# Two moves in the order of VectorE and ScalarE in a two-layer graph kernel

## The chip, the core and the metric

The kernel runs on one core of one Trainium2 chip. The metric is the device time of one launch in microseconds (us): the three runs of the kernel before gave 996.67, 996.7 and 994.24, median 996.67. The engines are named as the profile names them: PE is TensorE (PEld its weight loads), DVE is VectorE, ACT is ScalarE, POOL is GpSimd, SP is SyncE, which only issues transfers. Each engine runs its own instructions strictly in their order and waits on semaphores for the others.

## The reference

Inputs: x (8 x 2048 x 128), adj (2048 x 2048), W0 (128 x 128), W1 (3 x 128 x 128), bias (128), all fp32.

```
h = relu(layernorm(x))
A = relu((adj + adj.T) / 2);  d = rowsum(A) ** -0.5
x = x + relu(h @ W0 - d * (A @ (d * (h @ W0))))          # layer 0, per batch
h = relu(layernorm(x))
x = x + diag(adj) * (h @ W1[0]) + triu(adj, 1) @ (h @ W1[1])
      + tril(adj, -1) @ (h @ W1[2]) + bias               # layer 1, per batch
```

Layer 0 multiplies a symmetric 2048 x 2048 matrix by 8 batches of 2048 x 128, layer 1 does it with the two triangles of adj.

## The kernel before

**Tiling.** The 2048 rows are 16 strips of 128, the 8 batches two halves of 4, so one strip of one half is a tile of 128 x 512. A matmul in fp32 is split in three: each operand is written as a high part (suffix h, rounded to the fast type) and a low part (suffix l, the rest), and high x high, high x low and low x high are summed.

**Stages.** After a first phase (sums of rows and columns, h of half 0 and its product with W0) a step body runs 64 times, c = 0 to 63. A step makes one output strip of one half: 16 blocks k of three matmuls each into psAcc (lines 490 to 492), 48 in all. Steps 0 to 15 are layer 0 of half 0, 16 to 31 layer 0 of half 1, 32 to 47 and 48 to 63 layer 1 of the two halves. The matrix strip of a step comes in four quarters q of 128 x 512: C (from adj, or from DRAM once it is summed), Lh its high part (ACT, split_hi), Ll its low part (DVE, split_lo). In steps 0 to 15 PE also transposes adj (psA), ACT copies it (copy_T, AT), and DVE adds it to C (sum_T).

**Side work of a step.** PE does it between the blocks, in `finish(t, k)`:

- k = 3, steps 1 to 16: the transposed and normalised strip of half 1, yTh and yTl, times W0 into psW. ACT and DVE scale it into Yh and Yl.
- k = 7, steps 2 to 33: h2, the normalised result of the step before, is transposed into psZ (semaphore hT). ACT copies it into hTh (semaphore hThi), DVE makes hTl from psZ and hTh (hTlo).
- k = 11, steps 0 to 15: xp, a strip of half 1 that ACT has normalised (p_h), is transposed into the same psZ, and becomes yTh (ACT) and yTl (DVE). From step 2 on the transposes wait for hThi and hTlo.
- k = 11 and k = 14, steps 2 to 33: hTh and hTl times the three weights W1 into psG, 128 x 384 for each batch b. Batches 0 and 1 come at k = 11, 2 and 3 at k = 14. psG has two banks, b % 2, so batch 2 waits until bank 0 has been read (semaphore gev), batch 3 until bank 1 has.

**Who reads psG.** DVE adds the first 128 columns, times the diagonal, to x1: `t_out(t, b)`, line 797, semaphore tev. It waits for g_ok of the batch. ACT then copies the other 256 columns into g12: `gev_out(t, b)`, line 585, semaphore gev. It waits for tev of the same batch. t_dram and g_dram take both to DRAM for layer 1. The bias was added to x1 by POOL (xb_ok).

**The order around the change** is written out by hand in the bodies of ACT and DVE. ACT, in steps 2 to 15: split_hi, relu of z into x1 (line 611), Yh (614), normalisation of xp in four pieces (620), hTh (627), copy_T 1, split_hi 1, copy_T 2, the load of the next xp (638), yTh (640), gev_out 0 and 1, split_hi 2, h2 (651), gev_out 2 and 3. From step 16 on `prep(t)` (line 674) stands in the place of the xp normalisation: it copies xp, which then comes from g_dram, into the high operand of layer 1. DVE: x1 plus xe (840), Yl (844), hTl (849), sum_T 1, statistics of x1 (695 to 702), split_lo 1, yTl (859), t_out 0 and 1, sum_T 2, the negated mean (705), t_out 2 and 3.

Of the kernel before, what the change touches and what calls it, by code (L numbers as in the profile page):

```python
# [6 lines left out]
F32 = mybir.dt.float32  # L7
F32R = mybir.dt.float32r
ALU = mybir.AluOpType
ACT = mybir.ActivationFunctionType  # L10
# [4 lines left out]
NB = N // P  # L15
# [5 lines left out]
L1 = 2 * NB  # L21
# [19 lines left out]
def wait(eng, sem, value):  # L41

    if isinstance(value, int) and value <= 0:
        return
    eng.wait_ge(sem, value)
# [24 lines left out]
def build(nc, x, adj, w_l0, w_l1, bias, out):  # L70
# [12 lines left out]
    with ctx:  # L83
        def sb(name, shape, dt=F32, at=ctx):
            return at.enter_context(nc.sbuf_tensor(name, shape, dt))

        def sems(*names):
            return [ctx.enter_context(nc.semaphore(n)) for n in names]
# [26 lines left out]
        with ExitStack() as layer0:  # L115
# [8 lines left out]
        yTh, yTl = sb("yTh", [P, W], F32R), sb("yTl", [P, W], F32R)  # L124
        hTh, hTl = sb("hTh", [P, W], F32R), sb("hTl", [P, W], F32R)
# [22 lines left out]
        psZ = ctx.enter_context(nc.psum_tensor("psZ", [P, W], F32))  # L148
# [22 lines left out]
        yT, yThi, yTlo, yw_ok = sems("yT", "yThi", "yTlo", "yw_ok")  # L171
        cur_ok, hsum, z_ok, r1_ok, x1_ok = sems("cur_ok", "hsum", "z_ok", "r1_ok", "x1_ok")
        e_st, e_mv, e_ve, e_rs, e_nm, h2_ok, hT, hThi, hTlo = sems(
            "e_st", "e_mv", "e_ve", "e_rs", "e_nm", "h2_ok", "hT", "hThi", "hTlo")
        xb_ok, g_ok, gev, tev = sems("xb_ok", "g_ok", "gev", "tev")
# [20 lines left out]
        def blocks(ap):  # L196
            return ap.rearrange("p (b f) -> p b f", f=F)

        def strip(dram, s, back, q=None):

            a = dram[bass.ds(s.of(1, -back), 1)].rearrange("o p m -> (o p) m")
            return a if q is None else a[:, q * Q:(q + 1) * Q]
# [307 lines left out]
        def _(act):  # L510
            A = nc.scalar.activation
# [23 lines left out]
            def copy_T(s, q):  # L535

                wait(act, rT, s.of(4, q + 1))
                if q == 0:
                    wait(act, st_at[s.c % 2], s.pair(0, 16))
                A(AT[:, s.c % 2, q * Q:(q + 1) * Q], psA[:, q % 2, :], ACT.Copy).then_inc(at_ok, 1)  # L540

            def split_hi(s, q):

                if s.c < NB:
                    wait(act, S_ok, s.of(4, q + 1))
                else:
                    wait(act, ld_c[q], s.of(16, 16))
                if s.c:
                    wait(act, used, s.of(16, -16 + 4 * q + 4))
                A(Lh[:, q, :], C[:, q, :], ACT.Relu if s.c < L1 else ACT.Copy).then_inc(lhi, 1)  # L550
                if s.c < NB:
                    act.dma_start(strip(s_dram, s, 0, q), C[:, q, :]).then_inc(st_s[q], 16)
# [35 lines left out]
            def body(t):  # L588
                c = t.c
                pe_ = (c - 1) % 2  # L590
                nxt = Step(t.i, c + 1)
                if c:
                    split_hi(t, NQ - 1)
                if c >= L1:
                    wait(act, ld_lx, t.of(16, 16 * (1 - L1)))
                    wait(act, acc1, t.of(1, -L1))
                    A(lxh[:, :], lx[:, :], ACT.Copy).then_inc(lxh_ok, 1)
                    wait(act, ld_g2, t.of(16, 16 * (1 - L1)))
                    wait(act, slot_hi, t.of(1, -L1))
                    A(g2h[:, :], g2[:, :], ACT.Copy).then_inc(g2h_ok, 1)  # L600
                if c < NB - 1:
                    copy_T(nxt, 0)
                if c < LAST - 1:
                    split_hi(nxt, 0)
                if 1 <= c <= L1:
                    wait(act, z_ok, t.of(1, 0))
                    if c >= 3:
                        wait(act, st_t[pe_], t.pair(-1, 16))
                    elif c == 1:
                        act.wait_ge(wlo_ok, 1)  # L610
                    A(x1[:, pe_, :], z[:, :], ACT.Relu, scale=cur_e[:, 2:3]).then_inc(r1_ok, 1)
                if 1 <= c <= NB:
                    wait(act, yw_ok, t.of(1, 0))
                    A(Yh[:, bass.ds(t.of(1, -1), 1), :], psW[:, :].rearrange("p (o w) -> p o w", o=1), ACT.Copy,
                      scale=cur_e[:, 0:1]).then_inc(prep_hi, 1)
                if c < NB:
                    wait(act, p_nm, t.of(1, 1))
                    for b in range(HB):
                        f = slice(b * F, (b + 1) * F)
                        last = A(xp[:, f], xp[:, f], ACT.Relu, bias=npn.nm[:, b:b + 1], scale=npn.rs[:, b:b + 1])  # L620
                    last.then_inc(p_h, 1)
                elif c < L1 + NB:
                    prep(t)
                if 2 <= c < L1 + 2:
                    wait(act, hT, t.of(1, -1))
                    wait(act, g_ok, t.of(4, -8))
                    A(hTh[:, :], psZ[:, :], ACT.Copy).then_inc(hThi, 1)
                if c < NB - 1:
                    copy_T(nxt, 1)
                if c < LAST - 1:  # L630
                    split_hi(nxt, 1)
                if c < NB - 1:
                    copy_T(nxt, 2)
                if c < NB:
                    wait(act, yT, t.of(1, 1))
                    wait(act, yw_ok, t.of(1, 0))
                    if c < NB - 1:
                        act.dma_start(blocks(xp[:, :]), xv[1, bass.ds(t.of(1, 1), 1)]
                                      .rearrange("o p b f -> (o p) b f")).then_inc(ld_xp, 16)
                    A(yTh[:, :], psZ[:, :], ACT.Copy).then_inc(yThi, 1)  # L640
                if 2 <= c < L1 + 2:
                    gev_out(t, 0)
                    gev_out(t, 1)
                if c < LAST - 1:
                    split_hi(nxt, 2)
                if 1 <= c <= L1:
                    wait(act, e_nm, t.of(1, 0))
                    wait(act, hT, t.of(1, -1))
                    for b in range(HB):
                        f = slice(b * F, (b + 1) * F)  # L650
                        last = A(h2[:, f], x1[:, pe_, f], ACT.Relu, bias=ne.nm[:, b:b + 1], scale=ne.rs[:, b:b + 1])  # L651
                    last.then_inc(h2_ok, 1)
                if 2 <= c < L1 + 2:
                    gev_out(t, 2)
                    gev_out(t, 3)
                if c >= L1:
                    slot(t)
                if c < NB - 1:
                    copy_T(nxt, 3)
                if 2 <= c < L1 + 2:  # L660
                    wait(act, tev, t.of(4, -8 + 4))
                    act.dma_start(strip(t_dram, t, 2), x1[:, c % 2, :]).then_inc(st_t[c % 2], 16)
                    wait(act, gev, t.of(4, -8 + 4))
                    act.dma_start(strip(g_dram, t, 2), g12[:, :, :].rearrange("p k w -> p (k w)")).then_inc(st_g, 16)

            def prep(t):

                c = t.c
                dst, _ = half_of(c + NB)
                wait(act, ld_xp, t.of(16, 16))  # L670
                act.wait_ge(used, NB * (c // NB) * NB)
                wait(act, hsum, t.of(1, 1 - NB))
                off = t.of(1, -(c // NB) * NB)
                A(dst[:, bass.ds(off, 1), :], xp[:, :].rearrange("p (o w) -> p o w", o=1), ACT.Copy).then_inc(prep_hi, 1)  # L674

            def slot(t):
# [6 lines left out]
                  ACT.Copy).then_inc(slot_hi, 1)  # L683

            run_steps(act, body)


        @block.vector
        def _(dve):
            V = nc.vector  # L690
# [102 lines left out]
            def t_out(t, b):  # L793

                f = slice(b * F, (b + 1) * F)
                wait(dve, g_ok, t.of(4, -8 + b + 1))
                V.scalar_tensor_tensor(out=x1[:, t.c % 2, f], in0=psG[:, b % 2, 0:F], scalar=cur_g[:, 3:4],  # L797
                                       in1=x1[:, t.c % 2, f], op0=ALU.mult, op1=ALU.add).then_inc(tev, 1)

            def body(t):  # L800
                c = t.c
# [52 lines left out]
                    stats(ne, x1[:, pe_, :], e_st, e_mv, e_ve, t.of(1, 0))  # L854
                if c < LAST - 1:
                    split_lo(nxt, 1)
                if c < NB:
                    wait(dve, yThi, t.of(1, 1))
                    V.tensor_tensor(yTl[:, :], psZ[:, :], yTh[:, :].bitcast(F32), ALU.subtract).then_inc(yTlo, 1)
                if 2 <= c < L1 + 2:  # L860
                    wait(dve, xb_ok, t.of(1, -1))
                    t_out(t, 0)
                    t_out(t, 1)
                if c < NB - 1:
                    sum_T(nxt, 2)
                if 1 <= c <= L1:
# [150 lines left out]
```

## Time and profile before

| what | value |
|---|---|
| median of 3 runs | 996.67 us |
| lowest and highest | 994.24, 996.7 us |
| profiled execution | 995.62 us |
| its span | 993.9 us |
| PE busy | 940.1 us (95%) |
| DVE busy | 570.6 us (57%) |
| ACT busy | 501.3 us (50%) |
| POOL busy | 289.3 us (29%) |
| transfers | 213.73 MB, mean 215 GB/s |
| chain that ended last | PE 84%, issue 5%, ACT 3%, POOL 3% |

How to read it: busy time is the time in which an engine works on an instruction. A PE that is busy 95% of the span leaves little to win by faster work on the other engines; what counts there is where PE waits. The waits below are put down to the engine whose event came last. Releasers are inferred. In rows that merge several instructions, x4 is their number and the second column is the time from the first one's start to the last one's end. `[0.75 <-ACT g L585]` at a row's end is the idle time of the engine before it and what ended it. The profile writes x for x1, g for g12 and h for h2.

### The profile page before, as it was taken

How to read it: one execution, taken by the hardware profiler on the slowest of the kernel's cores; microseconds unless marked ns; L12 is line 12 of the kernel's file. 1: busy time of each engine (PE TensorE's matmuls, PEld its weight loads, DVE VectorE, ACT ScalarE, POOL GpSimd, SP SyncE). 2: the span in 40 equal slices, each digit the busy share in tenths (PEclk: the TensorE clock that was granted, in tenths of full speed). 3: DMA queues.
4: the chain of work that ended last, by engine and by line, in shares of the span. 5: the costliest groups of instructions: out<-in, count | busy, mean ns of one | idle time of the engine just before them, and what ended most of it. 6: DMA issues, size and time to landing. Idle time of an engine off the chain costs nothing.

```text
span 993.9 us, 17630 instructions
## 1 busy us (share of the span) xinstructions
PE 940.1 (95%) x4614; PEld 790.7 (80%) x4614; DVE 570.6 (57%) x1491; ACT 501.3 (50%) x1058; POOL 289.3 (29%) x289
## 2 busy tenths in 40 slices
PE   4787799999999999999999999999999999999998
PEld 4776688878878788888888887788888888888886
DVE  5996777667677676656666655453333433334342
ACT  5986566666656665445454554443343433333331
POOL 4776143433434334344443442111111100000000
PEclk9877899999999999999999999999999999999999
DMA  8995689889998987556565555675666655555552
GB/s 234 320 331 158 200 286 309 306 294 299 306 320 287 310 302 237 173 153 171 171 190 169 171 158 181 181 222 182 187 188 187 193 169 160 170 162 168 168 156 75
DMA packets 181210, 213.73 MB, mean 215 GB/s; under 512 B 13616, under 2 KB 116016, under 8 KB 178992
## 3 DMA queue, kind: packets, MB, share of 16 engines
q1 hardware_dynamic: 154816, 167.36, 55.8%
q10 hardware_dynamic: 26352, 45.88, 12.9%
q8 instruction: 18, 0.29, 0.1%
q14 instruction: 24, 0.20, 0.1%
HBM read 145.04 MB, written 68.16 MB: 215 GB/s over the span
## 4 chain that ended last, share of the span: by engine, by line
PE 84%; issue 5%; ACT 3%; POOL 3%; DVE 2%; DMA 1%; ACTq 1%; SPq 0%; DVEq 0%; POOLq 0%
PE psAcc L490 21%; PE psAcc L492 21%; PE psAcc L491 21%; PE psG L461 3%; PE psA L392 3%; PE psG L463 2%; PE psG L462 2%; PE psZ L423 2%; POOL colacc L918 2%; PE psA L404 1%; ACT yTh L640 1%; PE psW L364 1%; POOL n_rs L910 1%; PE psW L363 1%; PE psAcc L504 1%
## 5 line engine op out<-in xcount | busy, mean ns | idle before, releaser
L550 ACT ACTIVATE Lh<-C 128x512 fp32r<-128x512 f32 x256 | 161.4, 631 | 286.3 <-PE psAcc L492 236.2
L490 PE MATMUL psAcc<-Xh,Lh 128*128 128x512 f32 x512 | 208.0, 406 | 5.4 <-DVE Xl L777 4.7
L492 PE MATMUL psAcc<-Xh,Ll 128*128 128x512 f32 x512 | 201.9, 394 | 0.0
L491 PE MATMUL psAcc<-Xl,Lh 128*128 128x512 f32 x512 | 201.5, 394 | 0.0
L490 PE MATMUL psAcc<-Yh,Lh 128*128 128x512 f32 x512 | 200.9, 392 | 0.0
L492 PE MATMUL psAcc<-Yh,Ll 128*128 128x512 f32 x512 | 200.3, 391 | 0.0
L491 PE MATMUL psAcc<-Yl,Lh 128*128 128x512 f32 x512 | 200.0, 391 | 0.0
L721 DVE TENSOR_TENSOR Ll<-C,Lh 128x512 fp32r<-128x512 f32 x128 | 90.8, 711 | 143.6 <-ACT Lh L550 143.5
L490 PEld LDWEIGHTS psAcc<-Xh,Lh 128*128 128x128 f32 x512 | 97.7, 191 | 23.7 <-issue 6.3
L492 PEld LDWEIGHTS psAcc<-Xh,Ll 128*128 128x128 f32 x512 | 97.1, 190 | 21.3
L492 PEld LDWEIGHTS psAcc<-Yh,Ll 128*128 128x128 f32 x512 | 96.1, 188 | 20.2
L491 PEld LDWEIGHTS psAcc<-Xl,Lh 128*128 128x128 f32 x512 | 97.8, 191 | 17.8
L491 PEld LDWEIGHTS psAcc<-Yl,Lh 128*128 128x128 f32 x512 | 96.2, 188 | 18.9
L490 PEld LDWEIGHTS psAcc<-Yh,Lh 128*128 128x128 f32 x512 | 96.2, 188 | 18.7
L718 DVE SCALAR_TENSOR_TENSOR Ll<-C,Lh 128x512 fp32r<-128x512 f32 x128 | 95.9, 749 | 22.2 <-ACT Lh L550 19.6
L585 ACT ACTIVATE g<-psG 128x256 f32<-128x256 f32 x128 | 43.0, 377 | 68.4 <-DVE x L797 67.6
L976 POOL TENSOR_TENSOR x<-x,biasb 128x512 f32<-128x512 f32 x32 | 44.1, 1379 | 99.6 <-ACT h L651 99.6
L970 POOL TENSOR_TENSOR Yl<-xp,Yh 128x512 f32 (+1 forms) x16 | 20.7, 1292 | 162.6 <-ACT Yh L674 162.6
L910 POOL TENSOR_TENSOR ne_rs<-ne_ve,mhalf 128x4 f32<-128x4 f32 x32 | 44.8, 1400 | 75.5 <-DVE ne_ve L702 75.5
L797 DVE SCALAR_TENSOR_TENSOR x<-psG,cur_g,x 128x128 f32<-128x128 f32 x128 | 42.1, 347 | 40.0 <-PE psG L463 39.6
L712 DVE TENSOR_TENSOR C<-AT,C 128x512 f32<-128x512 f32 x64 | 46.9, 733 | 22.3 <-ACT AT L540 22.3
L540 ACT ACTIVATE AT<-psA 128x512 f32<-128x512 f32 x64 | 37.6, 590 | 43.2 <-PE psA L392 43.2
(124 smaller groups left out, 1469.8 us busy)
## 6 DMA issues: line engine op xcount, KB each, us to landing
C<-at_dram SPq DMA_DIRECT2D x128, 256.0 KB, 2.7
at_dram<-AT SPq DMA_DIRECT2D x16, 1088.0 KB, 5.5
R<-in_adj SPq DMA_DIRECT2D x64, 256.0 KB, 6.4
C<-in_adj SPq DMA_DIRECT2D x64, 256.0 KB, 4.8
s_dram<-C ACTq DMA_DIRECT2D x64, 256.0 KB, 4.3
g_dram<-g ACTq DMA_DIRECT2D x32, 512.0 KB, 4.2
C<-s_dram SPq DMA_DIRECT2D x64, 256.0 KB, 3.7
xe<-in_x SPq DMA_DIRECT2D x32, 256.0 KB, 3.7
```

The lines of the kernel that those rows point to most:

```text
L490: mm(acc, lh, rh[:, k, :], start=k == 0, stop=False)
L491: mm(acc, lh, rl[:, k, :], start=False, stop=False)
L492: mm(acc, ll, rh[:, k, :], start=False, stop=c < L1 and k == NB - 1).then_inc(used, 1)
L540: A(AT[:, s.c % 2, q * Q:(q + 1) * Q], psA[:, q % 2, :], ACT.Copy).then_inc(at_ok, 1)
L550: A(Lh[:, q, :], C[:, q, :], ACT.Relu if s.c < L1 else ACT.Copy).then_inc(lhi, 1)
L585: A(g12[:, :, b * F:(b + 1) * F], psG[:, b % 2, F:3 * F].rearrange("p (k f) -> p k f", k=2), ACT.Copy).then_inc(gev, 1)
L712: V.tensor_tensor(C[:, q, :], AT[:, s.c % 2, q * Q:(q + 1) * Q], C[:, q, :], ALU.add).then_inc(S_ok, 1)
L718: V.scalar_tensor_tensor(out=Ll[:, q, :], in0=C[:, q, :], scalar=0.0, in1=Lh[:, q, :].bitcast(F32), op0=ALU.max, op1=ALU.subtract).then_in ...
L721: V.tensor_tensor(Ll[:, q, :], C[:, q, :], Lh[:, q, :].bitcast(F32), ALU.subtract).then_inc(llo, 1)
L797: V.scalar_tensor_tensor(out=x1[:, t.c % 2, f], in0=psG[:, b % 2, 0:F], scalar=cur_g[:, 3:4], in1=x1[:, t.c % 2, f], op0=ALU.mult, op1=ALU ...
L910: return G.tensor_tensor(out=out, in0=base, in1=exponent, op=ALU.pow)
L976: G.tensor_tensor(out=blocks(x1[:, pe_, :]), in0=blocks(x1[:, pe_, :]), in1=biasb[:, :].unsqueeze(1).to_broadcast([P, HB, F]), op=ALU.add) ...
```

## The change

On ACT, the copy hTh moves ahead of the normalisation of xp (steps 2 to 15) and so ahead of `prep(t)` (steps 16 to 33). On DVE, t_out 0 and 1 move ahead of yTl in steps 2 to 15. From step 16 on yTl does not exist and DVE's order is the old one. No instruction is added or taken away, and every wait goes with its instruction.

```
@@ -613,6 +613,10 @@  (ScalarE)
+                if 2 <= c < L1 + 2:
+                    wait(act, hT, t.of(1, -1))
+                    wait(act, g_ok, t.of(4, -8))
+                    A(hTh[:, :], psZ[:, :], ACT.Copy).then_inc(hThi, 1)
                 if c < NB:
                     wait(act, p_nm, t.of(1, 1))
                     for b in range(HB):
...
                     last.then_inc(p_h, 1)
                 elif c < L1 + NB:
                     prep(t)
-                if 2 <= c < L1 + 2:
-                    wait(act, hT, t.of(1, -1))
-                    wait(act, g_ok, t.of(4, -8))
-                    A(hTh[:, :], psZ[:, :], ACT.Copy).then_inc(hThi, 1)
                 if c < NB - 1:
                     copy_T(nxt, 1)
@@ -854,13 +854,13 @@  (VectorE)
                 if c < LAST - 1:
                     split_lo(nxt, 1)
-                if c < NB:
-                    wait(dve, yThi, t.of(1, 1))
-                    V.tensor_tensor(yTl[:, :], psZ[:, :], yTh[:, :].bitcast(F32), ALU.subtract).then_inc(yTlo, 1)
                 if 2 <= c < L1 + 2:
                     wait(dve, xb_ok, t.of(1, -1))
                     t_out(t, 0)
                     t_out(t, 1)
+                if c < NB:
+                    wait(dve, yThi, t.of(1, 1))
+                    V.tensor_tensor(yTl[:, :], psZ[:, :], yTh[:, :].bitcast(F32), ALU.subtract).then_inc(yTlo, 1)
                 if c < NB - 1:
                     sum_T(nxt, 2)
```

VectorE in step 2, from the statistics of x1 to split_lo of quarter 2, before (x<-psG is t_out, C<-AT is sum_T, Ll is split_lo):

```order
L699 BN_AGGR ne_mv<-ne_st 128x2 x4
L702 TENSOR_SCALAR ne_ve<-ne_mv 128x4
L718 SCALAR_TENSOR_TENSOR Ll<-C,Lh 128x512
L859 TENSOR_TENSOR yTl<-psZ,yTh 128x512
L797 SCALAR_TENSOR_TENSOR x<-psG,cur_g,x 128x128 x2
L712 TENSOR_TENSOR C<-AT,C 128x512
L705 SCALAR_TENSOR_TENSOR ne_nm<-ne_mv,ne_rs 128x4
L797 SCALAR_TENSOR_TENSOR x<-psG,cur_g,x 128x128 x2
```

The same place after the change:

```order
L699 BN_AGGR ne_mv<-ne_st 128x2 x4
L702 TENSOR_SCALAR ne_ve<-ne_mv 128x4
L718 SCALAR_TENSOR_TENSOR Ll<-C,Lh 128x512
L797 SCALAR_TENSOR_TENSOR x<-psG,cur_g,x 128x128 x2
L863 TENSOR_TENSOR yTl<-psZ,yTh 128x512
L712 TENSOR_TENSOR C<-AT,C 128x512
L705 SCALAR_TENSOR_TENSOR ne_nm<-ne_mv,ne_rs 128x4
L797 SCALAR_TENSOR_TENSOR x<-psG,cur_g,x 128x128 x2
```

The first pair of t parts has changed places with yTl; the second pair stays.

ScalarE in step 2, from the relu to the first copies of psG, before (AT<-psA is copy_T, Lh is split_hi, g<-psG is gev_out):

```order
L611 ACTIVATE x<-z,cur_e 128x512
L614 ACTIVATE Yh<-psW,cur_e 128x512
L620 ACTIVATE xp<-xp,np_nm,np_rs 128x128 x4
L627 ACTIVATE hTh<-psZ 128x512
L540 ACTIVATE AT<-psA 128x512
L550 ACTIVATE Lh<-C 128x512
L552 DMA s_dram<-C 128x512
L540 ACTIVATE AT<-psA 128x512
L638 DMA xp<-in_x 128x4x128
L640 ACTIVATE yTh<-psZ 128x512
L585 ACTIVATE g<-psG 128x2x128 x2
```

The same place after the change, its first five instructions:

```order
L611 ACTIVATE x<-z,cur_e 128x512
L614 ACTIVATE Yh<-psW,cur_e 128x512
L619 ACTIVATE hTh<-psZ 128x512
L624 ACTIVATE xp<-xp,np_nm,np_rs 128x128 x4
L540 ACTIVATE AT<-psA 128x512
```

hTh now stands ahead of the four pieces of xp; what follows is unmoved.

## Rows read from the trace of the kernel before

**Rows 1.** Busy time of each engine: us, share of the span, instructions.

```profile
PE 940.1 (95%) x4614; PEld 790.7 (80%) x4614; DVE 570.6 (57%) x1491; ACT 501.3 (50%) x1058; POOL 289.3 (29%) x289
```

**Rows 2.** Waits, 136 to 390 us: engine, line, releaser: us, times, longest.

```profile
ACT AT L540 <- PE psA L392: 34.3, 26, 1.8
...
PE psG L461 <- ACT g L585: 9.1, 13, 0.8
PEld psZ L423 <- issue: 5.6, 11, 0.7
...
ACT x L611 <- DMA t_dram<-x: 2.0, 1, 2.0
...
DVE x L840 <- DMA xe<-in_x: 0.4, 1, 0.4
```

**Rows 3.** Timeline of PE, step 11, k = 14: start, us, instruction.

```profile
314.97 0.39 PE L492 MATMUL psAcc<-Xh,Ll 128*128 128x512 f32 x1
316.11 0.44 PE L461 MATMUL psG<-Wh,hTh 128*128 128x384 f32 x1 [0.75 <-ACT g L585]
316.38 0.33 PE L462 MATMUL psG<-Wl,hTh 128*128 128x384 f32 x1
```

**Rows 4.** Timeline of PE at the same place in step 19.

```profile
443.20 0.39 PE L492 MATMUL psAcc<-Yh,Ll 128*128 128x512 f32 x1
443.43 0.33 PE L461 MATMUL psG<-Wh,hTh 128*128 128x384 f32 x1
443.61 0.34 PE L462 MATMUL psG<-Wl,hTh 128*128 128x384 f32 x1
```

**Rows 5.** Timeline of ACT and DVE, step 11, around yTl.

```profile
313.98 0.60 ACT L640 ACTIVATE yTh<-psZ 128x512 fp32r<-128x512 f32 x1
...
314.61 0.69 DVE L859 TENSOR_TENSOR yTl<-psZ,yTh 128x512 fp32r<-128x512 f32 x1 [0.92 <-ACT yTh L640]
...
315.22 0.60 DVE L797 SCALAR_TENSOR_TENSOR x<-psG,cur_g,x 128x128 f32<-128x128 f32 x2
...
315.67 0.66 ACT L585 ACTIVATE g<-psG 128x256 f32<-128x256 f32 x2 [1.09 <-DVE x L797]
```

**Rows 6.** Timeline of ACT and DVE, step 11, around hTh.

```profile
308.18 1.64 ACT L620 ACTIVATE xp<-xp,np_nm,np_rs 128x128 f32<-128x128 f32 x4
...
309.72 0.58 ACT L627 ACTIVATE hTh<-psZ 128x512 fp32r<-128x512 f32 x1
...
310.33 0.69 DVE L849 TENSOR_TENSOR hTl<-psZ,hTh 128x512 fp32r<-128x512 f32 x1 [1.13 <-ACT hTh L627]
```

**Rows 7.** Timeline of PE, step 11, k = 11.

```profile
310.65 0.39 PE L492 MATMUL psAcc<-Xh,Ll 128*128 128x512 f32 x1
311.17 0.63 PE L423 MATMUL psZ<-ident,xp 128*128 128x128 f32 x4
```

**Rows 8.** Waits, 390 to 660 us.

```profile
ACT Xh L674 <- DMA xp<-g_dram: 26.8, 13, 3.4
...
PE psG L461 <- ACT hTh L627: 2.2, 1, 2.2
PE psG L461 <- DVE hTl L849: 1.0, 2, 0.8
```

**Rows 9.** Busy time by stretch: length, engines (instructions), granted clock, DMA share, GB/s.

```profile
308.30:309.30 1.00, 1.00 (x7) 0.79 (x6) 0.89 (x2) 1.00 (x3) 1.00 (x1) 1.00 0.06 12
...
312.30:313.30 1.00, 1.00 (x9) 0.97 (x8) 0.86 (x7) 0.07 (x1) 0.13 (x1) 1.00 1.21 426
...
620.93:624.35 3.42, 3.42 (x10) 2.82 (x9) 1.73 (x9) 2.05 (x6) 1.39 (x1) 0.51 0.33 97
```

**Rows 10.** Transfers, 136.24 to 373.35 us, all queues.

```profile
DMA packets 61043, 71.54 MB, mean 302 GB/s; under 512 B 3499, under 2 KB 42975, under 8 KB 59369
```

**Rows 11.** DMA issues, 300 to 318.9 us: KB each, us to landing.

```profile
xp<-in_x ACTq DMA_DIRECT2D x1, 256.0 KB, 6.5
```

**Rows 12.** Timeline of DVE, step 12: the statistics of xp.

```profile
320.62 0.86 DVE L695 BATCH_NORM_STATS2 np_st<-xp 128x6 f32<-128x128 f32 x4
```

More of the change, by code:

```diff
@@ L615, in body @@
                       scale=cur_e[:, 0:1]).then_inc(prep_hi, 1)
+                if 2 <= c < L1 + 2:
+                    wait(act, hT, t.of(1, -1))
+                    wait(act, g_ok, t.of(4, -8))
+                    A(hTh[:, :], psZ[:, :], ACT.Copy).then_inc(hThi, 1)
                 if c < NB:
@@ L623, in body @@
                     prep(t)
[L624 to L627, printed above, removed]
                 if c < NB - 1:
@@ L856, in body @@
                     split_lo(nxt, 1)
-                if c < NB:
-                    wait(dve, yThi, t.of(1, 1))
-                    V.tensor_tensor(yTl[:, :], psZ[:, :], yTh[:, :].bitcast(F32), ALU.subtract).then_inc(yTlo, 1)
                 if 2 <= c < L1 + 2:
@@ L863, in body @@
                     t_out(t, 1)
+                if c < NB:
+                    wait(dve, yThi, t.of(1, 1))
+                    V.tensor_tensor(yTl[:, :], psZ[:, :], yTh[:, :].bitcast(F32), ALU.subtract).then_inc(yTlo, 1)
                 if c < NB - 1:
```

## The prediction

> **What bounds the kernel now.** I read the busy times first. TensorE is busy 940.1 of 993.9 us [rows 1], so a change on VectorE or ScalarE pays only where TensorE waits. I split the span by step: one execution of the step body, which gives one strip of 128 rows of the result. The layer-0 steps c = 2 to 14 lie between 136.24 and 373.35 us, 13 steps of 18.24 us each. The steps from c = 34 on take about 11.6 us, and no moved instruction is in them. The waits of the stage come second [rows 2]. The reader should look for lines that start with PE or PEld, since the others are waits of engines that have time. Two matter. PE waits 9.1 us in 13 pieces for ACT's copy out of psG (L585), one piece per step. The weight loader stands idle 5.6 us in 11 pieces ahead of the transposes of xp (L423). "Issue" there means that the view names no releaser; I look for it below. The third view is the timeline of one step, c = 11, from 300 to 318 us.
>
> **Part 1, the t parts ahead of yTl on VectorE.** The chain is: t part b=0 (DVE L797) raises tev, ACT may then copy the same psG bank (L585), and PE may then write block b=2 into that bank (L461, at k = 14). Before, the last accumulating matmul starts at 314.97 and L461 at 316.11, which is 1.14 us later [rows 3]. Undisturbed, this pair is 0.23 us apart, and L462 follows L461 after 0.18, where behind the stall it takes 0.27 [rows 4]. A stall therefore costs more than the idle time shown: 1.14 - 0.23 = 0.91 against 0.75 shown, so 0.16 more, and 0.09 behind it.
> In [rows 5] DVE has nothing to do for 0.92 us before yTl: it waits for ACT's yTh (313.98 to 314.58), then does yTl (314.61 to 315.30), then the two t parts, and ACT's psG copies start at 315.67. The t parts need none of this. Their matmuls on b=0 and b=1 ended before 313. In the new order they run from about 313.6 to 314.2, inside the 0.92 us of idle time (0.60 us of work), and yTl still starts when yTh is done, at 314.6. So yTl pays nothing, and the sum_T behind it comes 0.4 us earlier. ACT finds tev raised when it is through with yTh, and copies b=0 from about 314.5 to 314.85. Before, PE's weight load started about 0.1 us after that copy; now it may start at 314.95, and PE is ready for it at about 315.2 (314.97 + 0.23). The stall goes, with a margin of 0.25 us. The second copy ends about 315.2 and is wanted at 315.8. What is late next at this place is yTh itself, which sits behind ACT's AT copy, and that copy waits for PE (the 34.3 us line of [rows 2]), so it moves along with PE.
> Term A: 9.1 + 13 x 0.16 + 13 x 0.09 = 12.4 us. Bounds: 0 if the wait only changes its name, 12.4 if it goes whole.
> Behind the stall ACT works without a gap until about 319.8 and can start only some 0.6 us earlier, not 1.0. It then has its waits for PE's transposes (34.3 us in the stage, 2.6 us per step), and they cover the 0.4 us.
>
> **Part 2, hTh ahead of the normalisation of xp on ScalarE, c < 16.** ACT runs relu x1, Yh, the four xp pieces (308.18 to 309.82) and then hTh (309.72 to 310.30); DVE waits 1.13 us and does hTl, 310.33 to 311.02 [rows 6]. PE's transposes of xp write psZ, which hTl reads, so they wait for it: the matmul before starts at 310.65 and the first transpose at 311.17, 0.52 us later [rows 7], against 0.23 undisturbed. The weight load follows hTl's end by 0.12 us. That is the "issue" of [rows 2].
> New: hTh at 308.2 to 308.8 (its source, the transposes of h2, is there by 307.9), xp from 308.7 to 310.3, hTl right behind Yl at about 309.1 to 309.8. PE then waits for xp: 310.3 + 0.12 = 310.4, wanted at 310.65. Margin 0.2 us, nothing paid for moving xp back by 0.5 us. ACT's total is the same, so its AT copy at 310.20 stays.
> Term B: 11 x 0.29 = 3.2 us. Bounds: if xp is late by the whole 0.5 us in every step, -13 x 0.3 = -3.9; if not, +3.2. I take 3.2, since the xp end is read from rows and only shifted by one copy.
>
> **Part 3, the same move in c = 16 to 33, ahead of the copy of the h operand (L674).** That copy waits up to 3.4 us for its DMA, with hTh behind it [rows 8]. PE shows this twice, 1.0 us in all; with 0.16 + 0.09 each 1.5 us. Once hTh goes first it is ready at its transposes' end, over 1 us before PE needs it. The L674 copy starts up to 0.6 us later in steps where its data are early. What waits for it is POOL's low part, which is needed only in the next stage. Term C: 1.5 us. At c = 32 PE waits 2.2 us for hTh [rows 8], but ACT is late there because of the g2 load; only the 0.6 us copy is taken out of its way, and DVE is not free for all of that. Term D: 0.3 us, bounds 0 and 0.6. Behind this wait the clock fell to half for 3.4 us (0.51 granted, [rows 9]), so 1.7 us more are possible if the shorter wait avoids it. I leave that out of the sum and keep it for the low end.
>
> **Transfers.** They are the cover that may go. The 13 steps move 71.54 MB at 302 GB/s [rows 10], 5.5 MB a step. At 18.24 - 1.2 = 17.0 us that is 323 GB/s. Single microseconds reach 426 GB/s, and there are holes with 12 [rows 9], about 2 us per step, so the same transfers fit in some 16.3 us.
> The Trainium skill (HBM Reference, the per-core bandwidth at its top) says a core alone streams at about 425 GB/s and that its share is about 358 when its neighbour streams too. The 426 above agrees with a core alone. By 425 a step's transfers would take 12.9 us, by 358 they would take 15.4, and both are under 17.0; the page speaks against the DMA rival below.
> Single landings are tight all the same. xp is issued at 313.51 and lands 6.5 us later [rows 11], 0.6 us before its statistics start at 320.62 [rows 12], and that interval shrinks by about 1.0. DVE then waits 0.4 us there, but it waits for an AT copy a little later in any case, which covers it. xe has some 2 us, t_dram's store 1.5; each has failed once already, 0.4 and 2.0 us [rows 2]. Term E: -1.5 us, an allowance for one or two such waits. Bounds 0 and -8.
>
> **Sum.** 12.4 + 3.2 + 1.5 + 0.3 - 1.5 = 15.9 us. The profiled execution took 995.62 us (span 993.9 and 1.7 around it) and would take 979.7. It lies 1.05 under the median of the three runs; from 996.67 the same sum gives 980.8. I predict 981.
>
> **Rivals.**
> (1) Transfers or a tight landing give part back. For it: the 302 GB/s mean of the stage [rows 10], and SP's queue, which waits for s_dram stores before it loads the next C. Against: the holes. If each of 13 steps loses 0.5 us, the time is 981 + 6.5 = 987.5, near 988.
> (2) The margins of 0.2 us do not hold: yTh or xp ends just late, and PE waits for them instead. A wait of 0.3 us with its 0.25 of extra in each of 13 steps, at one of the two places, gives 7 us back: also 988. At both places: 995, no change.
> (3) The change does not do what it says at L461, because PE's wait hangs on something other than tev, such as the g_dram store that the b=0 copy also waits for. Against: that store is issued about 301.1 and lands 5 to 6 us later, long before 314.5. Only B, C and D would be left: 996.7 - 5 = 992.
> (4) Slower: SP's queue becomes the bound. It is in order, so a late s_dram store holds up xe and the loads behind it; a late xe holds up DVE, hence hTl and PE. It decides when the landing times of 4.7 to 6.5 us grow by over 2 us. To end above 999.7 it must take back the 17.4 and 3 more, 1.6 us in each step, so a step of 18.6 us with less data in flight than now. The price is possible, the profile gives it little.
>
> **Chances.** Forecast (976 to 984.5) 0.66; rivals 1 and 2 (984.5 to 990) 0.22; rival 3 and larger parts of 1 and 2 (990 to 993.7) 0.06; no change 0.03; slower 0.03. The 0.3% that a measurement of this kernel tells from no change is 3 us. Faster: 0.66 + 0.22 + 0.06 = 0.94. The range 976 to 989 leaves out the upper cases, about 0.14, and a little at the low end: C, A and B whole, no allowance and the clock kept gives 996.67 - 17.4 - 1.7 = 977.6.
>
> **What the profile after should show.** The line PE psG L461 <- ACT g gone or under 2 us, yTl's wait for yTh down from 0.92 to about 0.3 us per step, the psG copies right behind yTh; hTl without its wait for hTh in both stages; the load before the xp transposes without its "issue"; steps of about 17.0 us; 320 GB/s or more over the stage. Wrong if: PE waits for ACT xp L624 or ACT yTh in most steps (rival 2), new DMA waits on DVE L840, L695 or ACT L611 (rival 1), or the L461 wait stays (rival 3). If steps are 17.0 us and the total is not 14 us or more lower, the loss is in the stages I took as unchanged.

## The result and the profile after

| kernel | median, us | lowest to highest | ratio to before, 95% interval |
|---|---|---|---|
| before | 996.35 (4 runs) | 994.24 to 996.7 | 1 |
| changed | 978.35 (4 runs) | 977.53 to 980.24 | 0.9826 (0.9806 to 0.9847) |

The change takes 18.0 us off. The forecast was 981, with 976 to 989 as the range. In a second set of runs, on another chip, the changed kernel stood at 977.21 against 996.9, ratio 0.9797 (0.9773 to 0.9821).

The profiled execution of the changed kernel took 980.24 us, the slowest of its four, with a span of 978.5. Before it was 995.62 and 993.9. So the two traces differ by 15.4 us and the medians by 18.0. The difference is cut up below by the start of `z` (DVE L813) or of the result (L891), which happens once in each step.

| stretch, us | before | changed | difference |
|---|---|---|---|
| first phase and step 0 | 120.57 | 121.89 | +1.32 |
| step 1 | 15.67 | 15.69 | +0.02 |
| steps 2 to 14 | 237.11 | 222.83 | -14.28 |
| steps 15 to 31 | 236.91 | 235.01 | -1.90 |
| steps 32 and 33 | 38.18 | 37.46 | -0.72 |
| steps 34 to 63 | 341.80 | 342.00 | +0.20 |

The sum is -15.4. The first row is scatter, not the change: over the twelve profiles of this study, none of whose edits touches the first phase, it lies between 117.8 and 123.1 us. What an edit does is therefore read from the stretches, and the total only from the runs.

The busy times of the changed kernel answer to [rows 1]. PE is busy 6.5 us less, at the same share of 95%. Of this 4.8 us lie in steps 2 to 14, where the matmul before a stall is counted to its own end (0.39 us) and not to the next start (0.23 us), and 1.8 us in steps 32 and 33, where the kernel before had 3.4 us at the lower clock.

```profile
PE 933.6 (95%) x4614; PEld 793.2 (81%) x4614; DVE 568.6 (58%) x1491; ACT 504.1 (52%) x1058; POOL 285.7 (29%) x289
```

The waits of the changed kernel from 136 to 373 us (engine, line, releaser: us, times, longest) answer to [rows 2]:

```profile
ACT AT L540 <- PE psA L392: 27.5, 26, 1.6
...
DVE yTl L863 <- ACT yTh L640: 3.6, 13, 0.4
DVE x L840 <- DMA xe<-in_x: 2.7, 3, 0.9
...
DVE np_st L695 <- DMA xp<-in_x: 1.6, 3, 0.9
...
ACT x L611 <- DMA t_dram<-x: 1.4, 1, 1.4
...
PEld psZ L423 <- ACT xp L624: 1.1, 1, 1.1
PE psZ L423 <- DVE hTl L849: 0.9, 2, 0.7
```

PE's 9.1 us for the psG copies are gone, and so is the "issue" ahead of L423 but for one. yTl's wait is 3.6 us, 0.28 a step. DVE waits longer for transfers, 2.7 us for xe where it was 0.4, and two of these waits reach PE, in steps 5 and 7 (0.68 and 0.20 us of idle time at L423); the wait for xp L624 is in step 5 too.

The timeline of the changed kernel at k = 14 of step 11 (start, us, instruction) answers to [rows 3, 5]:

```profile
305.19 0.60 DVE L797 SCALAR_TENSOR_TENSOR x<-psG,cur_g,x 128x128 f32<-128x128 f32 x2
305.37 0.60 ACT L640 ACTIVATE yTh<-psZ 128x512 fp32r<-128x512 f32 x1
305.86 0.66 ACT L585 ACTIVATE g<-psG 128x256 f32<-128x256 f32 x2
306.00 0.69 DVE L863 TENSOR_TENSOR yTl<-psZ,yTh 128x512 fp32r<-128x512 f32 x1 [0.20 <-ACT yTh L640]
...
306.37 0.40 PE L492 MATMUL psAcc<-Xh,Ll 128*128 128x512 f32 x1
306.60 0.34 PE L461 MATMUL psG<-Wh,hTh 128*128 128x384 f32 x1
306.77 0.34 PE L462 MATMUL psG<-Wl,hTh 128*128 128x384 f32 x1
```

The t parts run beside yTh, the psG copies start 0.49 us after yTh does instead of 1.69, and L461 follows L492 after 0.23 instead of 1.14. L462 follows after 0.17, not 0.27.

The timeline of the same step around k = 11 answers to [rows 6, 7]:

```profile
299.88 0.59 ACT L619 ACTIVATE hTh<-psZ 128x512 fp32r<-128x512 f32 x1
...
300.35 1.65 ACT L624 ACTIVATE xp<-xp,np_nm,np_rs 128x128 f32<-128x128 f32 x4
...
300.81 0.68 DVE L849 TENSOR_TENSOR hTl<-psZ,hTh 128x512 fp32r<-128x512 f32 x1
...
302.35 0.40 PE L492 MATMUL psAcc<-Xh,Ll 128*128 128x512 f32 x1
302.58 0.49 PE L423 MATMUL psZ<-ident,xp 128*128 128x128 f32 x3
```

hTh is done at 300.47. hTl no longer waits for it, only for DVE's own Yl, and is done at 301.49. xp is done at 302.00, 0.35 us before the last matmul ahead of the transposes starts, and the transposes come 0.23 after that matmul. With the 0.12 us that the prediction puts between an operand's end and the weight load, the margin is 0.23 us.

Busy time by stretch for the changed kernel: length, PE, PEld, DVE, ACT, POOL (instructions), granted clock, DMA share, GB/s. The next row is its transfer total over steps 2 to 14; it answers to [rows 10].

```profile
137.58:360.41 222.83, 221.95 (x1247) 192.95 (x1246) 171.02 (x507) 146.14 (x312) 90.34 (x117) 1.00 0.95 322
360.41:595.42 235.01, 235.01 (x1122) 199.89 (x1121) 144.88 (x406) 125.25 (x266) 98.37 (x74) 1.00 0.59 179
```

```profile
DMA packets 61123, 71.71 MB, mean 322 GB/s; under 512 B 3505, under 2 KB 42973, under 8 KB 59449
```

The same 71.7 MB go through in 222.8 us. In steps 15 to 31 PE's busy time equals the length of the stretch.

### The profile page after: what moved, and what is told of

It is laid out like the page before. It is cut to its first block, busy times and chain, and to the rows that moved or that the text cites. A ratio compares the mean times of both kernels' runs of the same rounds, so it can differ in the third digit from the quotient of the medians.

```text
span 978.5 us, 17630 instructions
## 1 busy us (share of the span) xinstructions
PE 933.6 (95%) x4614; PEld 793.2 (81%) x4614; DVE 568.6 (58%) x1491; ACT 504.1 (52%) x1058; POOL 285.7 (29%) x289
## 4 chain that ended last, share of the span: by engine, by line
PE 84%; issue 4%; DMA 3%; DVE 3%; ACT 3%; POOL 1%; SPq 0%; ACTq 0%; DVEq 0%; POOLq 0%
PE psAcc L492 22%; PE psAcc L490 22%; PE psAcc L491 22%; PE psA L392 2%; PE psG L461 2%; PE psG L463 2%; PE psG L462 2%; PE psZ L423 2%; DMA s_dram<-C 1%; DMA xe<-in_x 1%; PE psA L404 1%; ACT hst L521 1%; PE psAcc L504 1%; PE psAcc L503 1%; PE psAcc L502 1%
## 5 line engine op out<-in xcount | busy, mean ns | idle before, releaser
L492 PE MATMUL psAcc<-Xh,Ll 128*128 128x512 f32 x512 | 201.1, 393 | 0.0
L492 PE MATMUL psAcc<-Yh,Ll 128*128 128x512 f32 x512 | 200.1, 391 | 0.0
L492 PEld LDWEIGHTS psAcc<-Xh,Ll 128*128 128x128 f32 x512 | 96.8, 189 | 21.2
L492 PEld LDWEIGHTS psAcc<-Yh,Ll 128*128 128x128 f32 x512 | 96.1, 188 | 20.2
L976 POOL TENSOR_TENSOR x<-x,biasb 128x512 f32<-128x512 f32 x32 | 41.9, 1308 | 91.9 <-ACT h L651 91.9
L891 DVE TENSOR_TENSOR x<-psAcc,x 128x512 f32<-128x512 f32 x32 | 22.1, 691 | 59.7 <-PE psAcc L504 46.6
```

What stands on the lines that cost most here:

```text
L492: mm(acc, ll, rh[:, k, :], start=False, stop=c < L1 and k == NB - 1).then_inc(used, 1)
L891: V.tensor_tensor(x1[:, pp, :], psAcc[:, pp, :], x1[:, pp, :], ALU.add).then_inc(o_ok, 1)
L976: G.tensor_tensor(out=blocks(x1[:, pe_, :]), in0=blocks(x1[:, pe_, :]), in1=biasb[:, :].unsqueeze(1).to_broadcast([P, HB, F]), op=ALU.add) ...
```

## The experiments

All ratios are to the kernel before on the same chip. Two numbers are counted from each trace over steps 2 to 14. "k = 14" is the sum of the start-to-start times L492 to L461 above 0.23 us, plus those of L461 to L462 above 0.18. "k = 11" is the sum of L492 to L423 (xp) above 0.23. The kernel before had 996.16 on the chip of the next four rows after "changed", 994.82 on that of the four after them, and 996.9 on that of the last two, so medians of different chips are compared through the ratio.

| kernel | median | ratio (95%) | steps 2 to 14 | k = 14 | k = 11 | steps 15 to 31 | 32 and 33 |
|---|---|---|---|---|---|---|---|
| before | 996.35 | 1 | 237.11 | 12.4 | 3.0 | 236.91 | 38.18 |
| changed | 978.35 | 0.9826 (0.9806 to 0.9847) | 222.83 | 0 | 1.2 | 235.01 | 37.46 |
| VectorE part alone | 982.04 | 0.9862 (0.9841 to 0.9883) | 224.78 | 0 | 3.1 | 237.34 | 37.01 |
| ScalarE part alone | 989.59 | 0.9947 (0.9926 to 0.9967) | 233.86 | 12.4 | 0 | 235.01 | 36.48 |
| old order from step 16 | 980.98 | 0.9849 (0.9826 to 0.9873) | 221.76 | 0 | 0.1 | 237.56 | 37.18 |
| yTh in 4 pieces | 976.95 | 0.9809 (0.9787 to 0.9831) | 223.44 | 0 | 2.1 | 235.01 | 37.01 |
| yTh in 8 pieces | 980.77 | 0.9862 (0.9843 to 0.9880) | 224.02 | 2.8 | 0.3 | 234.98 | 36.20 |
| xe loaded early | 978.01 | 0.9828 (0.9808 to 0.9848) | 221.59 | 0 | 0 | 235.02 | 37.44 |
| lxh, g2h late | 975.03 | 0.9810 (0.9791 to 0.9829) | 222.60 | 0 | 1.0 | 235.02 | 34.87 |
| the last two together | 974.29 | 0.9801 (0.9783 to 0.9819) | 221.65 | 0 | 0 | 235.02 | 34.90 |
| changed, again | 977.21 | 0.9797 (0.9773 to 0.9821) | 221.85 | 0 | 0.3 | 235.02 | 36.30 |
| the last two, again | 975.47 | 0.9784 (0.9759 to 0.9808) | 221.66 | 0 | 0 | 235.02 | 35.15 |

**The VectorE part alone.**

```
-                if c < NB:
-                    wait(dve, yThi, ...); V.tensor_tensor(yTl...)
                 if 2 <= c < L1 + 2:
                     wait(dve, xb_ok, t.of(1, -1))
                     t_out(t, 0)
                     t_out(t, 1)
+                if c < NB:
+                    wait(dve, yThi, ...); V.tensor_tensor(yTl...)
```

> Only the first two t parts move ahead of yTl on VectorE; ScalarE as before. My theory (two independent stalls of TensorE per step, one at k = 14 behind the psG copies, one at k = 11 behind hTl): the k = 14 stall goes, 12.4 us less than before over steps 2 to 14, the k = 11 stall stays at 0.2 to 0.3 us a step. About 984 to 985 us; PE psG L461 <- ACT g under 1 us in the stage, DVE hTl <- ACT hTh unchanged near 15 us. Rival (the two moves need each other, since either stall alone can hold the step): less than half of it, 990 or more, with the k = 11 wait grown to 0.8 us or more a step.

Measured: 982.04 us, steps 2 to 14 shorter by 237.11 - 224.78 = 12.33 us, the 12.4 that was expected. The total is 2 us below what was expected, within its interval (0.9841 to 0.9883 is 4 us wide). The k = 11 stall is untouched. Its waits, 136 to 362 us:

```profile
DVE hTl L849 <- ACT hTh L627: 12.7, 11, 1.2
...
PEld psZ L423 <- issue: 5.7, 11, 0.8
```

The rival, that one stall alone can hold the step, falls: at k = 11 PE waits as long as before, 3.1 against 3.0 us.

**The ScalarE part alone.** The changed ScalarE with the old VectorE, so the diff is the first hunk of the change.

> Only hTh moves ahead on ScalarE; VectorE as before. My theory: terms B, C and D alone, 3.2 + 1.5 + 0.3 to 0.7 us, so 991 to 992 us; the k = 14 stall stays at 0.7 to 0.9 us in 13 steps. Rival (what PE gains at k = 11 it loses at k = 14, because the psG copies hang on VectorE's yTl and do not move): the steps 2 to 14 stay at 18.2 us and only C and D are left, 994 to 995 us; the k = 14 stall would then grow to about 1.1 us.

Measured: 989.59 us. Steps 2 to 14 are 3.25 us shorter, and the k = 11 stall is down from 3.0 to 0. The k = 14 stall has not grown (12.4 both times), so the rival that PE loses there what it gains at k = 11 falls. The stretches show 3.25 + 1.90 + 1.70 = 6.9 us; 991 to 992 was expected. The two last steps gave more than the 0.3 to 0.7 expected. Its waits, 136 to 375 us:

```profile
PEld psG L461 <- ACT g L585: 14.6, 13, 1.2
...
PE psG L461 <- ACT g L585: 8.9, 13, 0.8
```

The parts add up but for the late landings: 12.33 + 3.25 = 15.58 alone, 14.28 together, and the missing 1.3 is the k = 11 column of the changed kernel (1.2).

**The old order from step 16.**

```
+                if 2 <= c < NB:
+                    ... hTh
                 if c < NB:
                     ... xp
                 elif c < L1 + NB:
                     prep(t)
+                if NB <= c < L1 + 2:
+                    ... hTh
```

> The changed kernel, but from step 16 on hTh stands behind the copy of the h operand again. My theory: steps 2 to 14 as in the changed kernel (17.1 us each), steps 15 to 31 give back 1.5 to 1.9 us, and at c = 32 the wait of PE for hTh is 2.2 us again, with the half clock behind it (up to 1.7 us): 980 to 982 us. Rival (the later part of the move is worth nothing and the gain there was a chance of landing times): 978 to 979 us, and steps 15 to 31 as long as in the changed kernel.

Measured: 980.98 us, steps 15 to 31 at 237.56, 2.55 us longer than in the changed kernel. Each kernel with the new order from step 16 has 235.0 there (nine profiles, 234.98 to 235.02), and each without it 236.9 to 237.6 (three profiles). The rival falls. PE's waits of this kernel, 390 to 660 us:

```profile
PE psG L461 <- ACT hTh L631: 2.0, 1, 2.0
...
PE psG L461 <- DVE hTl L853: 1.1, 3, 0.5
```

The 2.0 us wait at step 32 is back as expected, but no half clock follows it, and steps 32 and 33 take 37.18 us, no longer than in the changed kernel.

**yTh in four pieces.** A delay of the psG copies without other work:

```
-                    A(yTh[:, :], psZ[:, :], ACT.Copy).then_inc(yThi, 1)
+                    for k in range(4):
+                        f = slice(k * 128, (k + 1) * 128)
+                        last = A(yTh[:, f], psZ[:, f], ACT.Copy)
+                    last.then_inc(yThi, 1)
```

> The changed kernel with the copy yTh cut into four pieces of 128 columns, so that it ends later by some 0.3 us (if a piece takes 0.23) to 1.0 us (if it takes the 0.4 of the xp pieces), and the psG copies behind it too. The margin at k = 14 was forecast as 0.25 us. My theory: with a delay of d the stall is back at d - 0.25 a step plus 0.25 of extra once it exists, so for d = 0.3 about 0.3 x 13 = 4 us (982), for d = 1.0 about 13 us (991). Rival (the margin is much larger, since PE is not at L461 before 315.5): no change for d = 0.3, 978 to 979.

Measured: the four pieces take 0.79 us, and the psG copies start 0.65 us after yTh does instead of 0.49. So d is 0.16, less than either case the expectation gave, and inside the margin: no stall at k = 14, no change of time. By itself it decides nothing.

**yTh in eight pieces** of 64 columns, the same edit.

> The changed kernel with the copy yTh cut into eight pieces of 64 columns. Cut into four it cost 0 to 0.2 us of PE's margin at k = 14 and no time. Eight pieces at the same step should end about 0.8 us later than the one copy. My theory (margin 0.25 us, then the stall is back): about 0.5 us a step in 13 steps, 6 to 8 us more than the changed kernel, 984 to 986 us, with PE psG L461 <- ACT g back in 12 or 13 steps. Rival (PE has much more room there): 978 to 979 us and no such wait.

Measured: 1.04 us for the eight, the psG copies 0.84 us after the start of yTh, so d is 0.35. The stall is back in the ten steps of the loop, the steps with the small margin. Its timeline, step 11:

```profile
304.47 1.04 ACT L642 ACTIVATE yTh<-psZ 128x64 fp32r<-128x64 f32 x8
305.31 0.75 ACT L585 ACTIVATE g<-psG 128x256 f32<-128x256 f32 x2
...
305.46 0.40 PE L492 MATMUL psAcc<-Xh,Ll 128*128 128x512 f32 x1
305.83 0.44 PE L461 MATMUL psG<-Wh,hTh 128*128 128x384 f32 x1
306.12 0.34 PE L462 MATMUL psG<-Wl,hTh 128*128 128x384 f32 x1
```

L461 comes 0.37 us after L492, 0.14 late, and L462 0.11 late behind it. So the margin is 0.35 - 0.14 = 0.2 us; 0.25 was forecast. The cost is 2.8 us by the k = 14 column and 3.6 by the ratios (0.9862 against 0.9826, whose intervals just overlap). The 6 to 8 expected was wrong mainly in d, taken as 0.8. The price of a step was taken as d - 0.25 and is d - 0.2 + 0.1, in ten steps and not 13.

**xe loaded early.** SP asks for xe right after the store of AT, ahead of the loads for the step after next:

```
+                if c < L1:
+                    step_wait(sp, x1_ok, t.of(1, 0))
+                    ... sp.dma_start(xe)
                 for q in range(1, NQ):
                     if c < LAST - 2:
                         load_next(Step(t.i, c + 2), q - 1)
...
-                    if q == 2 and c < L1:
-                        ... the same load
```

> The changed kernel with the load of xe issued by SP ahead of two loads of the step after next (R and C of quarters 0 and 1), some 8 us earlier. My theory (what is left over 17.0 us in steps 5 and 7 is a late xe): DVE x <- DMA xe gone, steps 5 and 7 as long as their neighbours, steps 2 to 14 down from 222.8 to 221.5 us, total 1 to 1.5 us less: 977. Rival (the transfers as a whole are the limit, and xe only the one that shows): another landing takes its place, xp or t_dram, and steps 2 to 14 stay at 222.8 or above.

In the changed kernel, step 5, the chain from xe to PE reads (timeline; the add L840 itself takes 1.15 us here and 0.69 in step 11, of which more in the last section):

```profile
197.06 1.15 DVE L840 TENSOR_TENSOR x<-x,xe 128x512 f32<-128x512 f32 x1 [0.93 <-DMA xe<-in_x]
...
198.80 0.67 DVE L849 TENSOR_TENSOR hTl<-psZ,hTh 128x512 fp32r<-128x512 f32 x1
...
199.62 0.63 PE L423 MATMUL psZ<-ident,xp 128*128 128x128 f32 x4 [0.68 <-DVE hTl L849]
```

With the early load the only wait for a transfer left from 136 to 375 us is this, and it reaches nobody:

```profile
DVE np_st L695 <- DMA xp<-in_x: 0.8, 2, 0.5
```

Steps 2 to 14 are 221.59 us and the k = 11 column is 0, as in both other profiles with this edit. The six with the VectorE and the ScalarE part and xe in its old place have 0.1 to 2.1 there, so the chain is shown, and what it costs differs from one execution to the next. The rival falls too, since nothing took its place. In the total the version can't be told from the changed kernel (978.01, ratio 0.9828 against 0.9826).

**lxh and g2h late**, in steps 32 and 33 only: on ScalarE both copies move behind hTh, on VectorE lxl and g2l behind hTl.

```
-                if c >= L1:
+                if c >= L1 + 2:
                     ... lxh, g2h       (lxl, g2l on VectorE)
...
+                if L1 <= c < L1 + 2:
+                    ... lxh, g2h       (lxl, g2l, behind hTl)
```

> The changed kernel with the copies of the diagonal block and of g2 (lxh, g2h on ScalarE, lxl, g2l on VectorE) behind hTh and hTl in steps 32 and 33 only. My theory (TensorE waits at k = 11 of these two steps because hTh stands behind copies that wait for a load issued at the step's start): the waits of 1.5 and 1.1 us go, steps 32 and 33 together 37.5 to 35 us, total 2 to 2.5 us less, 976. Rival (the same loads gate the end of the step, so that the wait only moves there): the two steps stay at 37 us or more.

Measured: 975.03 us, the two steps at 34.87 instead of 37.46. In the changed kernel hTh started at 602.83 only, behind copies that had waited 4.8 us for lx, and PE stood 1.45 us at L461. Of PE's waits from 590 to 640 us in the changed kernel,

```profile
PE psG L461 <- issue: 2.5, 2, 1.5
PE psAcc L490 <- issue: 1.4, 1, 1.4
PE psAcc L490 <- DVE Xl L883: 0.4, 1, 0.4
```

the first is gone with the edit and the other two stay:

```profile
PE psAcc L490 <- issue: 1.4, 1, 1.4
PE psAcc L490 <- DVE Xl L896: 0.4, 1, 0.4
```

The theory holds for the place. The waits did not move to the end of the step. The size is less sure: the repeat of the changed kernel has 36.30 us in the two steps without the edit, so it is worth 1.4 to 2.6 us, and the totals (0.9810 against 0.9826) lie within each other's intervals.

**Both edits, and a last comparison.**

> Both of the last two edits on the changed kernel. My theory: the gains add, 1.3 + 2.5 us less than the changed kernel, about 974.5 us. Rival: one of them gives nothing, 976 to 978 us.

> The changed kernel once more, as the yardstick on the same chip for the kernel with both later edits. My theory: 18 us under the kernel before, ratio 0.982 to 0.983; steps 2 to 14 at 222 to 223 us, steps 15 to 31 at 235.0. Rival (the step sums of the first profile were a lucky execution): steps 2 to 14 at 224 us or more and a ratio of 0.985.

> The kernel with xe loaded early and lxh, g2h behind hTh, on the same chip as the changed kernel. My theory: 1.2 us less in steps 2 to 14 and 2.6 us less in steps 32 and 33, 3.5 to 4 us under the changed kernel. Rival (the difference of 4 us seen across two chips was mostly scatter): under 2 us.

Measured: 974.29 us, on a chip where before had 994.82, 1.5 us less than on the chip of the changed kernel. That it meets the 974.5 expected is partly luck of the chip: the ratio of 0.9801 times 996.35 is 976.5, which is in the rival's range. On a third chip the changed kernel has 977.21 and the version with both edits 975.47, 1.7 us less, where 3.5 to 4 were expected; the intervals of the ratios overlap. That is the rival's "under 2 us" in the total. The stretches agree with the theory in the place and not in the size: steps 32 and 33 are 1.15 us shorter there (36.30 to 35.15), 2.6 in the earlier pair, and steps 2 to 14 had almost nothing left to give in that execution (0.2). The version is the fastest by median in both sets. That it beats the changed kernel is probable and not shown by the totals: the ratios differ by 2.5 us in one pair and 1.3 in the other, inside their intervals.

## Why the prediction was right

**Term A, 12.4 us, bounds 0 and 12.4.** Measured 12.33 with this part alone. It came out because the stall was counted by starts, not by the idle time shown: the page's 9.1 us leave out 0.16 a step, in which the modelled end of a matmul runs over the next start, and 0.09 of the slower matmul behind. By the waits view alone the forecast would have been 3.3 us short. The instructions did what was written: t parts in DVE's idle time, psG copies at once behind yTh, margin 0.2 for 0.25.

**Term B, 3.2 us.** Measured 3.25 alone. The view named no releaser ("issue"); that it was hTl was read from one step's timeline and is confirmed, since the 3.0 us went with the ScalarE part and not with the VectorE part. The lower bound, xp late by 0.5 us in each step, did not come: the margin was 0.23 us where 0.2 was forecast.

**Term C, 1.5 us.** Measured 1.9 to 2.5. The term was sized from the wait lines, which gave 1.0 us in two pieces. Counted by starts, as terms A and B were, before has four such stalls in steps 15 to 31 (steps 19, 20, 23, 27), 1.54 us at L492 to L461 and 0.37 behind, together the 1.9 that went. The same count gives 2.3 and 2.6 us in the two other profiles with the old order, and none with the new one. DVE's wait for hTh in 390 to 660 us is still there, 27.6 us after 40.4 before: now it ends with the transposes, not with a load.

**Term D, 0.3 us, with 1.7 more left out for the clock.** This is the worst-sized term. One reading behind it was wrong: ACT is late at step 32 because of the load of lx, for which it waited 5.36 us, and not of g2 (0.36 us). Steps 32 and 33 took 38.18 us before and 36.2 to 37.5 in the kernels with hTh first, but the two other profiles with the old order have 37.0 and 37.2. So before's 38.18 holds about 1 us that was its own. The two traces show of what it is made. From L461 of b = 0 to L461 of b = 2 PE took 4.77 us before, with the half clock of [rows 9], and 3.20 changed, so the clock cost 1.6 us. But in the changed kernel PE waits 1.35 us at the start of step 33, 0.27 before, which takes 1.1 us of it back. This wait is 1.35 to 1.38 us in all eleven other profiles, also with the VectorE part alone and with the old order, so the ScalarE move did not bring it. Just ahead of it the trace of the changed kernel shows

```profile
609.88 1.50 DVE L883 CAST Xl<-g2l 128x512 fp32r<-128x512 f32 x1
...
611.59 0.47 PE L490 MATMUL psAcc<-Xh,Lh 128*128 128x512 f32 x1 [1.35 <-issue]
```

and that of the kernel before

```profile
627.06 0.42 DVE L883 CAST Xl<-g2l 128x512 fp32r<-128x512 f32 x1
...
627.69 0.47 PE L490 MATMUL psAcc<-Xh,Lh 128*128 128x512 f32 x1 [0.27 <-ACT Xh L682]
```

At the start of step 33 PE waits for both halves of this slot, ACT's L682 and DVE's L883. The view names ACT before, but L682 had ended at 627.35 and L883 only at 627.48. PE starts 0.21 us after the end of L883 in both, and 0.21 to 0.24 in all twelve profiles. So the wait is for DVE's copy, which took 1.50 us instead of 0.42; the last section shows beside what. The wait at step 32 itself went from 2.24 us before, and 1.9 and 2.0 in the other two with the old order, to 1.4 to 1.8 with hTh first: the 0.3 forecast is of the right size for that.

**Term E, -1.5 us for landings.** 1.2 us in the profiled execution, by the path that was named (xe, then hTl, then PE), 0.1 to 0.3 in three others with both parts of the change and xe in its old place, 1.0 in the one with lxh and g2h late and 2.1 in the one with yTh in four pieces. xp's late landings, 1.6 us in three pieces, cost nothing, as forecast. The allowance was a little large for most of them.

**The sum.** 15.9 was forecast. The three changed stretches of the profiled execution give 16.9, those of the repeat 15.26 + 1.89 + 1.88 = 19.0, and the medians 18.0. Of the 2.65 us between 981 and 978.35, 0.55 are the base (996.67 - 15.9 = 980.77, rounded up, and a fourth run put the median of before at 996.35). The other 2.1 can be C (0.4 to 1.0), D (0.4 to 1.6) and E (0.3 to 1.4), but the interval of the ratio is 4 us wide, so the totals don't divide them. One side reading was off and nothing hangs on it: the steps from 34 on take 11.4 us (341.80 / 30), not 11.6.

**The rivals.** (1) was real in kind and small in size: its sign, DVE waiting for xe and xp, came in 3 of 13 steps each. 322 GB/s were reached, with the DMA share at 0.95, and the total transfers did not bind. The Trainium skill (HBM Reference, at its top) gives about 425 GB/s for a core alone and about 358 beside a busy neighbour; 322 lies under both and tests neither. (2) did not come, but eight pieces of yTh show how near it is: 0.2 us. (3) fell, since the L461 wait vanished whole with tev's earlier raising. (4) was not seen: on SP's path the longest landing of xe in steps 2 to 14 was 7.3 us before and 6.3 changed, and the medians of all its loads stayed within 0.3 us.

## What to carry to other kernels

On an in-order engine, ask of each instruction that another engine waits for whether what stands ahead of it is itself waiting: two of the three gains here came out of idle time that sat in front of ready work. Count a TensorE stall from start to start against the same pair undisturbed, because the idle time shown was a quarter too small. Before an order is changed, write down the margin of each new last arrival; here both were about 0.2 us, and both held in nearly every step that no late transfer touched. The same count belongs to the small terms: C, sized from the two waits that the view listed, came out at 1.5 us for at least 1.9.

## What the runs showed of the hardware that was not expected

**VectorE beside GpSimd.** The slot copy L883 (a cast of 128 x 512) took 0.42 us in 373 executions of the instruction, and 1.50 us in the 11 that started while POOL's add of the bias (L976 in the changed kernel) was running, also 128 x 512. There it ended 0.28 to 0.29 us after POOL's add did:

```profile
609.45 1.64 POOL L976 TENSOR_TENSOR x<-x,biasb 128x512 f32<-128x512 f32 x1 [2.20 <-ACT h L651]
```

The add of xe (L840) shows the same. It takes 0.69 us, but in the 15 cases of these profiles in which it started while POOL's add into z (L963 in the changed kernel) was running it ended 0.54 to 0.55 us after that, whenever it had started, and took up to 1.79 us. 13 of the 15 come right behind a wait of 0.3 us or more for xe. So here a late transfer cost DVE more than its lateness: 0.93 us of wait and 0.46 of a longer add in step 5 of the changed kernel.

**The clock.** A wait of PE of 2.24 us at step 32 was followed by 3.4 us at the half level of the clock (1.2 instead of 2.4 GHz) in the profile before. The same wait at 2.04 us (old order from step 16) and 1.88 us (VectorE part alone), and at 1.39 to 1.82 us in the six profiles with hTh first, was followed by none. The half level cost 1.6 us in the one profile that has it, of which the slot copy gave 1.1 back. Whether the other executions of before had it too no trace shows, so its part in the 18 us of the medians stays open.

**Scatter and pieces.** The first phase with step 0, which is all but the same in every kernel here, took between 117.8 and 123.1 us in twelve executions, more than the whole effect of several edits, while steps 15 to 31 agreed within 0.04 us among the nine kernels with the new order. A copy out of PSUM by ScalarE took 0.60 us in one piece of 512 columns, 0.79 in four and 1.04 in eight: about 0.06 us for each further piece.
